# A selective-scan chunk relaid: 14 late products on GpSimd, a residual sum on TensorE, and gate logits from raw rows

## The reference

```python
def step(h, inp):                      # the scan over time
    dt_t, B_t, C_t, u_t = inp
    dA = jnp.exp(dt_t[..., None] * A)
    h = h * dA + (dt_t * u_t)[..., None] * B_t[:, None, :]
    y = jnp.einsum('bes,bs->be', h, C_t)
    return (h, y)
...
y = tm(ys) + x_conv * D
y = y * silu(z)
return jnp.einsum('bte,de->btd', y, out_proj_w)
...
x = x + mamba(rmsnorm(x), ...)
h = jnp.square(jax.nn.relu(c_fc(rmsnorm(x))))
x = x + c_proj(h)
...
x = x + 0.5 * ffn(layernorm(x))        # before: logits = layernorm(x) @ gate_w.T + gate_b, softmax, top 2
x = x + attn(layernorm(x))             # the block above; its inner x is layernorm(x)
x = x + 0.5 * ffn(layernorm(x))
```

## Time and profile before

| | us |
|---|---|
| median of 3 runs | 1990.0 (1989.86 to 1990.74) |
| profiled execution | 1994.02 |
| its span, first to last instruction | 1992.2 |
| mean granted TensorE clock | 0.931 |
| first gate and slots | 0 to 98 |
| experts, first time | 98 to 506 |
| mamba: up to the first scan | 506 to 563.8 |
| mamba: scan stage | 563.8 to 1492.7 |
| mamba: the rest, and the second gate | 1492.7 to 1545 |
| second route and experts | 1545 to 1992 |

### The profile page before, as it was taken

The page is one execution under the profiler, slowest core; times in us unless marked ns, Lnnn a source line. Parts: engine busy times, 40 slices in busy tenths (PEclk is TensorE's granted clock), DMA queues, the critical chain, the costliest instruction groups (busy, mean ns, idle before and its releaser), DMA issues. The chain is left out here.

```text
span 1992.2 us, 31078 instructions
## 1 busy us (share of the span) xinstructions
PE 1681.0 (84%) x10860; PEld 1389.6 (70%) x10860; DVE 1615.9 (81%) x2722; ACT 974.2 (49%) x1641; POOL 1290.3 (65%) x799
## 2 busy tenths in 40 slices
PE   6479999996578698888989888998787399999996
PEld 6379999996245465556556555655665299999996
DVE  5657867766469999999999999999997677777675
ACT  1323333332266676676777767676652433333331
POOL 1047646547368888878888887888862356555455
PEclk9989999998779899899989999899888699999998
DMA  6344434442444444445444444445432734344331
GB/s 203 97 116 106 95 78 93 86 80 39 147 139 140 153 137 156 142 135 155 135 151 147 144 155 134 154 138 160 138 112 74 227 75 98 81 91 91 78 69 23
DMA packets 161099, 237.59 MB, mean 119 GB/s; under 512 B 29482, under 2 KB 85408, under 8 KB 160416
## 3 DMA queue, kind: packets, MB, share of 16 engines
...
...
## 5 line engine op out<-in xcount | busy, mean ns | idle before, releaser
L1519 POOL TENSOR_TENSOR m_dB<-m_DTU,m_BC 128x1024 f32<-128x1024 f32 x256 | 603.1, 2362 | 153.9 <-DVE m_HS L1615 78.3
L1615 DVE TENSOR_TENSOR_SCAN PS<-PS,m_ST,m_dB 128x512 f32<-128x512 f32 x448 | 552.7, 1271 | 25.8 <-POOL m_dB L1519 25.1
L1272 ACT ACTIVATE PS<-m_DT,m_A 128x512 f32<-128x512 f32 x512 | 332.1, 681 | 195.4 <-DVE m_ST L1631 195.0
L1247 PEld LDWEIGHTS PS<-keep_ident,m_G 128*128 128x128 f32 x2048 | 252.7, 149 | 153.9 <-issue 69.4
L1247 PE MATMUL PS<-keep_ident,m_G 128*128 128x128 f32 x2048 | 292.3, 288 | 56.2 <-POOL m_G L1508 36.4
L1622 DVE TENSOR_TENSOR m_G<-PS,m_BC 128x512 f32<-128x512 f32 x448 | 297.6, 671 | 0.0
L623 PE MATMUL PS<-e_xh,e_wh 128*128 128x256 f32 x1008 | 290.3, 288 | 0.0
L680 ACT ACTIVATE e_hh<-e_u 128x512 fp32r<-128x512 f32 x252 | 156.4, 633 | 270.6 <-DVE e_u L736 267.3
L623 PE MATMUL PS<-e_xl,e_wh 128*128 128x256 f32 x1008 | 284.6, 282 | 0.0
L623 PE MATMUL PS<-e_xh,e_wl 128*128 128x256 f32 x1008 | 284.4, 282 | 0.0
L641 PE MATMUL PS<-e_wh,e_hh 128*128 128x256 f32 x1008 | 281.4, 279 | 0.0
...
## 6 DMA issues: line engine op xcount, KB each, us to landing
m_BC<-bc_rows SPq DMA_DIRECT2D x512, 256.0 KB, 3.8
...
```

Source lines behind the costliest of these rows:

```text
L1247: last = M(PS[:, B_Y + j, ts], G[:, n % NG, j, ts], C["ident"][:, :], is_transpose=True, start=False, stop=(s == DS - 1 and a == CTT - 1))
L1272: return nc.scalar.activation(out, in_, func, **kw)
L1519: G_.tensor_tensor(dB[:, s % 2, :, :], DTU[:, es, :], BC[:, s % NBC, 0:1, :].to_broadcast([P, 2, CT]), ALU.mult).then_inc(dB_ok, 1)
L1615: V.tensor_tensor_scan(HS[:, :] if on_pool(n, j) else state(n, j), state(n, j), dB[:, s % 2, j, :], ST[:, s, e:e + 1], ALU.mult, ALU.add). ...
```

## The change

- **First gate.** The loads of X move from `route` into `setup`, behind its three small loads. PE transposes rows of `X` itself, as soon as a quarter is there, and waits for the centred gate only before the first logits. DVE multiplies all logits by rstd in one more instruction. `xn` is still made and stored, and no longer waits for PE.
- **Products.** `on_pool` takes every odd step but the last of each half: 14 of a chunk's 32 second products instead of 8, and POOL makes them three steps later in its queue. PE adds such a product two steps late (`LAG`), so a G buffer that held one is free two steps later. `dB` has three buffers, `HS` two, and `sp1` lies in `XR` and `hT` instead of a buffer of its own.
- **Rows of C** are fetched one step later than rows of B.
- **Residual sum.** xa is gone from POOL. pj starts with one more product with the identity, of `XP`.
- **Layout.** The front of a chunk starts earlier (xr at 0 instead of 2, T at 2, x at 4, 6, 8, 10, c at 7, 9, 12, 14); silu goes from 15 to 16; z 1 to 3 from 26, 29, 30 to 21, 23, 26. sz goes from step 15 of its own chunk to step 28 of the chunk before (chunk 0: step 4), followed by a load of the exponential's table.

```diff
-            if x_dram is not None:
-                for q in range(4):
-                    sp.dma_start(X[:, q * Q:(q + 1) * Q, :],
-                                 x_dram[q * Q * P:(q + 1) * Q * P, :].rearrange("(t p) d -> p t d", p=P)).then_inc(x_in[q], 16)
...
-                    dve.wait_ge(tp_ok, h * NX + (g + 1))
...
+                dve.wait_ge(rstd_ok, QUARTERS)
+                link(V.tensor_tensor(lg[:, :, :], lg[:, :, :], bc(rstd), ALU.mult))
...
-                pe.wait_ge(centred, 1)
...
-                        pe.wait_ge(xn_ok, h * NX + (pair + g + 1))
+                        pe.wait_ge(x_in[(h * NX + pair + g) // 2], 16)
...
                                 last = nc.tensor.transpose(PS[:, 2 * g + k, a * P:(a + 1) * P],
-                                                           xn[:, pair + g, a, k * P:(k + 1) * P], C["ident"][:, :])
+                                                           X[:, (h * NX + pair + g) * 4 + a, k * P:(k + 1) * P], C["ident"][:, :])
...
+                        if h + pair + g == 0:
+                            pe.wait_ge(centred, 1)
...
-        dB = sb("dB", [P, 2, 2, CT])
+        NDB = 3
+        dB = sb("dB", [P, NDB, 2, CT])
...
-        sp1 = sb("sp1", [P, 2, CT])
+
+        sp1 = (XR[:, :, :].rearrange("p (j h) d -> p j (h d)", j=2), hT[:, :, :])
...
-            return j == 1 and n % 4 == 1
-
-        SHARED = STEPS // 4
+            return j == 1 and n % 2 == 1 and n % DS < DS - 1
+
+        SHARED = STEPS // 2 - PAIRS
+        LAG = 2
+
+        def g_free(k, n, j):
+
+            return k * STEPS + n - NG + 1 + (LAG if on_pool((n - NG) % STEPS, j) else 0)
...
         LATE = {
             ("dt", 2): (0, 1, _, _), ("dt", 3): (3, 4, _, _), ("sp", 1): (_, 6, _, _), ("add", 1): (_, _, _, 10),
-            ("du", 1): (_, _, _, 13), ("sz", 0): (_, 15, _, _), ("g", 0): (18, 19, _, _), ("g", 1): (18, 19, _, _),
-            ("xn", 0): (_, 30, _, _),
+            ("du", 1): (_, _, _, 13), ("sz", 0): (_, _, _, _), ("g", 0): (18, 19, _, _), ("g", 1): (18, 19, _, _),
+            ("xn", 0): (_, 31, _, _),
         }
         EARLY = {
-            ("xr", 0): (_, 2, _, _), ("T", 0): (4, 5, _, _), ("T", 1): (5, 6, _, _), ("x", 0): (7, 8, _, _), ("x", 1): (8, 9, _, _),
-            ("c", 0): (9, 10, _, _), ("c", 1): (10, 11, _, _), ("x", 2): (11, 12, _, _), ("x", 3): (12, 13, _, _), ("c", 2): (13, 14, _, _),
-            ("c", 3): (14, 15, _, _), ("silu", 0): (_, 15, _, _), ("z", 0): (17, 18, _, _), ("xp", 0): (19, 20, _, _),
-            ("dt", 0): (21, 22, _, _), ("dt", 1): (22, 23, _, _), ("sp", 0): (_, 24, _, _), ("z", 1): (26, 27, _, _),
-            ("add", 0): (_, _, _, 28), ("du", 0): (_, _, _, 30), ("z", 2): (29, 30, _, _), ("z", 3): (30, 31, _, _),
+            ("xr", 0): (_, 0, _, _), ("T", 0): (2, 3, _, _), ("T", 1): (2, 3, _, _), ("x", 0): (4, 6, _, _), ("x", 1): (6, 8, _, _),
+            ("c", 0): (7, 9, _, _), ("x", 2): (8, 10, _, _), ("c", 1): (9, 11, _, _), ("x", 3): (10, 12, _, _), ("c", 2): (12, 14, _, _),
+            ("c", 3): (14, 16, _, _), ("silu", 0): (_, 16, _, _), ("z", 0): (17, 18, _, _), ("xp", 0): (19, 20, _, _),
+            ("dt", 0): (21, 22, _, _), ("dt", 1): (22, 23, _, _), ("sp", 0): (_, 24, _, _), ("z", 1): (21, 22, _, _),
+            ("add", 0): (_, _, _, 28), ("du", 0): (_, _, _, 30), ("z", 2): (23, 24, _, _), ("z", 3): (26, 27, _, _),
         }
         BACK = {
-            ("g", 2): (1, 2, _, _), ("g", 3): (2, 3, _, _),
-            ("out", 0): (4, 5, _, _), ("out", 1): (6, 7, _, _), ("sq", 0): (_, 8, _, _), ("v", 0): (_, _, _, 14),
-            ("hr", 0): (_, 14, _, _), ("xa", 0): (_, _, _, 16), ("hT", 0): (15, 16, _, _), ("hT", 1): (16, 17, _, _), ("xa", 1): (_, _, _, 18),
+            ("g", 2): (1, 2, _, _), ("g", 3): (1, 2, _, _),
+            ("out", 0): (3, 5, _, _), ("out", 1): (5, 7, _, _), ("sq", 0): (_, 8, _, _), ("v", 0): (_, _, _, 12),
+            ("hr", 0): (_, 13, _, _), ("hT", 0): (15, 16, _, _), ("hT", 1): (17, 18, _, _), 
             ("fc", 0): (20, 21, _, _), ("fc", 1): (23, 24, _, _), ("fc", 2): (24, 25, _, _), ("q", 0): (_, 25, _, _),
-            ("fc", 3): (25, 26, _, _), ("q", 1): (_, 26, _, _), ("pj", 0): (27, 28, _, _), ("pj", 1): (28, 29, _, _),
+            ("fc", 3): (25, 26, _, _), ("q", 1): (_, 26, _, _), ("pj", 0): (27, 29, _, _), ("pj", 1): (28, 30, _, _),
         }
...
+        SEND_AT, GATES_AT = 26, 28
...
+            def load(at, j):
+
+                k, n = divmod(at, STEPS)
+                old_k, old_n = divmod(at - NBC, STEPS)
+                if at >= NBC:
+                    if j == 0:
+                        sp.wait_ge(dB_ok, at - NBC + 1)
+                    else:
+                        if on_pool(old_n, 1):
+                            wait_product(sp, old_k, old_n, 1)
+                            sp.sem_inc(c_free, 1)
+                        wait_product(sp, old_k, old_n, 0 if on_pool(old_n, 1) else 1)
+                src = bc_dram[k:k + 1, j, n % DS:n % DS + 1, :].rearrange("o q t -> (o q) t")
+                sp.dma_start(BC[:, at % NBC, j, :], src.to_broadcast([P, CT])).then_inc((c_in if j else b_in)[at % NBC], 16)
...
+                        at = k * STEPS + p * DS + s
+                        load(at, 0)
+                        if at > 0:
+                            load(at - 1, 1)
...
-                        pe.wait_ge(xa_ok, k * 2 + (n + 1 + XA0))
+                        wait_read(pe, k, ("out", n), into=p)
...
+                    if kind == "pj":
+                        M(bank(p, k), C["ident"][:, :], XP[:, 2 * n:2 * n + 2, :].rearrange("p t d -> p (t d)"), start=False, stop=False)
...
-                        for j in range(2):
-                            wait_product(pe, k, n, j)
+                        for m, j in ((n, 0), (n - LAG, 1), (n, 1)):
+                            if s < LAG and m != n or on_pool(m % STEPS, j) != (m != n):
+                                continue
+                            wait_product(pe, k, m, j)
                             for a in range(CTT):
                                 ts = slice(a * P, (a + 1) * P)
-                                last = M(PS[:, B_Y + j, ts], G[:, n % NG, j, ts], C["ident"][:, :], is_transpose=True,
-                                         start=False, stop=(s == DS - 1 and a == CTT - 1))
+                                last = M(PS[:, B_Y + j, ts], G[:, m % NG, j, ts], C["ident"][:, :], is_transpose=True,
+                                         start=False, stop=(s == DS - 1 and m == n and a == CTT - 1))
...
+                    exp_set()
...
-                    act.wait_ge(xa_ok, k * 2 + XA0)
+                    if not is_first(k):
+                        wait_written(act, ("pj", 1), k - 1)
...
-                        if n == LATE["sz", 0][ON_ACT] and not has_front:
-                            exp_set()
+                        if n == GATES_AT and has_front:
+                            front(("sz", 0), k + 1, 1 - par)
+                        elif n == 4 and is_first(k):
+                            front(("sz", 0), 0, 0)
...
-                elif kind == "xa":
-                    wait_read(gp, k, ("out", n))
-                    x = X[:, bass.ds(k * CTT + 2 * n, 2), :]
-                    G_.tensor_tensor(x, x, XP[:, 2 * n:2 * n + 2, :], ALU.add).then_inc(xa_ok, 1)
...
+                    gp.wait_ge(g_read, g_free(k, n, 1))
+                G_.tensor_tensor(G[:, n % NG, 1, :], HS[:, on_pool_before(n) % 2, :], BC[:, n % NBC, 1, :], ALU.mult).then_inc(p_ok, 1)
...
+                        at = k * STEPS + n
+                        if at >= NDB:
+                            gp.wait_ge(scanned, 2 * (at - NDB + 1))
+                        G_.tensor_tensor(dB[:, at % NDB, :, :], DTU[:, es, :], BC[:, s % NBC, 0:1, :].to_broadcast([P, 2, CT]),
                                          ALU.mult).then_inc(dB_ok, 1)
-                        if n >= 2 and on_pool(n - 2, 1):
-                            weigh(k, n - 2)
+                        if n >= NDB and on_pool(n - NDB, 1):
+                            weigh(k, n - NDB)
+                        elif n < NDB and k > 0 and on_pool(STEPS + n - NDB, 1):
+                            weigh(k - 1, STEPS + n - NDB)
...
+            def last_products():
+                for n in range(STEPS - NDB, STEPS):
+                    if on_pool(n, 1):
+                        weigh(MCH - 1, n)
+
+            run(gp, turn, front, back, last_products, between)
...
+                            so_far = k * SHARED + on_pool_before(n)
+                            if on_pool(n, j) and so_far >= 2:
+                                dve.wait_ge(p_ok, so_far - 1)
+                                dve.wait_ge(p_kept, so_far - 1)
+                            V.tensor_tensor_scan(HS[:, on_pool_before(n) % 2, :] if on_pool(n, j) else state(n, j), state(n, j), dB[:, (k * STEPS + n) % NDB, j, :], ST[:, s, e:e + 1],
```

(6 more changed lines are left out.)

56 lines of the change are left out of this document (15 added, 41 removed), and 2 rows, old and new, of the table ROWS_AT.

## The result

The changed kernel takes **1975.6 us** (median of 8 runs, 1966.1 to 1977.2) against 1987.3 us for the kernel before on the same chip (8 runs, 1979.3 to 1990.7); the ratio is **0.9938, 95% interval 0.9914 to 0.9961**. It is faster, but the forecast of 1938 us and its range, 1929 to 1960, both missed. The forecast also took the median of the runs to lie 4.0 us under the profiled execution, as it did before; behind the change it lies 1.0 us above it, and that alone is 5 of the 37.6 us by which the median was missed.

A forecast was written before the change was run, and what follows sets the result against it. The scan stage was taken as bound by DVE's instruction stream plus 23.2 us of waits. Profiled 1994.0 - 28.8 - 15.2 - 9.6 + 1.7 = 1942.1 us; the median, 4.0 lower, was forecast at 1938 us, range 1929 to 1960.

The forecast's parts named there:

- Term 4: First gate: transposing raw rows of X lets PE begin 10.1 us earlier, less one added multiplication: -9.6 us.
- Term 1: Scan stage: six more second products per chunk move from DVE to POOL, 0.60 us each over 8 chunks: -28.8 us.
- a third dB buffer lets POOL run about 5 us ahead: Scan stage, dB(10) to dB(14): POOL's lead over DVE covers its queue with a margin of about 0.3 us.
- Term 2: Scan stage: DVE's waits of 23.2 us shrink to 8 us as sz moves to an earlier step: -15.2 us.
- the remainder: DVE waits still left in the scan stage: 8 us, 1 us a chunk, with bounds 0 and 23.2 us.
- the squares end about 2.6 us into step 27: Before step 31: from there two pj groups and accumulations 27 to 29 need some 13 us, of 13.2 us.
- Steps 15 and 31: Two waits said to get tighter: DVE's product there waits for PE's step n-2 instead of n-4.
- Term 3: Residual sum on PE: two more products of 0.86 us per chunk, exposed only after the last chunk: +1.7 us.
- PE becomes the bound: Rival, scan stage: PE's work plus 100.1 us of rigid idle time gives 904.5 us, total 1957.5; chance 0.17.
- dB-paced: Rival, scan stage: POOL has no real slack and each DVE step waits for dB: 1967 us; chance 0.05.
- The table load cost no drain: Rival on sz's table loads on ACT: each switch costs a drain too, about 2.66 us: 1953 us; chance 0.03.

The follow-up runs named there:

- s_start: The kernel before with only the new start (X loads in setup, raw rows transposed, logits scaled afterwards): 1973.3 us, ratio 0.9932.
- p_taps: The changed kernel with two of the four taps of the convolution left out, so less TensorE work at steps 7 to 14: 1957.7 us, ratio 0.9841.
- w_pool: The changed kernel with GpSimd's first-half work spread out (dt3, softplus, add and du at earlier steps): 1962.7 us, ratio 0.9858.
- g_lag1: The changed kernel with LAG = 1 instead of 2 and nothing else: 1949.1 us, ratio 0.9818.

## Why the forecast was wrong, step by step

- **Term 4, the start (-9.6): right.** At equal speed of the logits it is 10.3 us (553.5 in s_start); transposes began at 9.72, 9.8 was forecast. The other 2.5 us of the 12.8 are luck of this execution: one of its four groups of logits ran in 4.19 us, not 6.83. The softmax stood at 48.14 and not near 51 for that reason.
- **Term 1, the products moved (-28.8): its arithmetic right, its worth not.** VectorE's busy time fell by 27.6 us, nearly as counted (905.8 to 878.2). The step that failed is the sentence "a third dB buffer lets POOL run about 5 us ahead", with its margin of about 0.3 us. GpSimd's queue was walked from dB to dB without the wait *in front of its own products*, for their G buffer. That wait spent 3.84 us of the lead before step 10, and VectorE waited 2.7 us a chunk, 18.5 in all. No row of before could show it, but the diff did: `g_free` adds LAG on GpSimd's side too.
- **Term 2, the remainder (8 us): mis-sized at the place it named.** The step was the sum that starts at "the squares end about 2.6 us into step 27" and gives "some 13 us, of 13.2 us", taken as just enough. The squares ended 4.5 us into step 27, since they stand behind fc3 on a TensorE that was already late. From there to the end of accumulation 29 it took 14.7 us and not 13, since z3 and accumulation 26 still stood ahead of the first pj group: the squares ended at 1108.82, the group began at 1110.27. So step 31 waited 3.4 to 3.5 us in five chunks (20.9 us with the others). A count that lands on the line is a wait, and each chunk pays it. Steps 15 and 31 were both named as tighter; step 15 never waited; that the dB waits ahead of it had slowed VectorE down is the likely reason, and no run tried it. That the gate leaves ACT's chain was right: no wait for it is left.
- **Term 3 (+1.7): right for what it counted.** Behind the scans the two new products take 0.86 us each (one in each pj group), 1.7 together, as forecast. The tail grew by 3.1; the other 1.4 us go with a slower clock behind the scans (granted 0.83 against 0.86), which is not shown to be their cause. In the stage TensorE's busy time is 806.9, and 804 was forecast. What the residual sum costs in the stage was not tried alone.
- **The rivals.** "PE becomes the bound" gave 904.5 us for the stage and named its sign, VectorE waiting 25 us or more. It waited 41.7 us, and yet neither size nor cause fit: the stage took 919.9, and p_taps shows that TensorE's amount of work isn't it. "dB-paced" named the right wait and the wrong reason, slack of GpSimd, which w_pool and g_lag1 exclude. The table load cost no drain: a load at 1111.91, sz at 1113.21, the load back at 1115.14 and the decay at 1116.43 are 1.30 and 1.29 us a switch, and decays waited 0.6 us in the whole stage. There the Trainium skill (ScalarE: Activation LUTs, section What ACT_TABLE_LOAD costs), with its 2.66 us a switch, is not borne out.

So the cause is settled in its main part: LAG = 1 alone gives back 19.4 of the 34.9 us missed in the stage, 13 products with LAG = 1 and filler 23.9. The last 11 us stay open; in that kernel they lie in waits of 0.2 to 1.5 us at the gates and of 0.7 us at step 15.
